# Masked attention: who adds the mask of two of the four score blocks

## The reference, cut to what matters

```
Q, K, V = proj(q, w_q), proj(k, w_k), proj(v, w_v)        # 16 heads of 16
scores = einsum('bhqd,bhkd->bhqk', Q, K) / sqrt(16)
scores = where(mask == 0, -1e9, scores)
attn = softmax(scores, axis=-1)
out = einsum('bhqk,bhkd->bhqd', attn, V) ... @ w_o.T
```

## Time and profile before

| | us |
|---|---|
| median of 3 runs | 1202.81 |
| lowest, highest | 1201.06, 1209.94 |
| the profiled execution, own time | 1203.75 |
| its span in the trace | 1202.0 |
| PE busy over the span | 1050.5 (87%) |
| DVE, ACT, POOL busy over the span | 659.1 (55%), 636.5 (53%), 200.0 (17%) |

### The profile page before, as it was taken

How to read it: one execution, slowest core, us unless ns; L and a number is a source line. 1 busy time by engine, 2 the same in 40 slices (tenths; PEclk the granted TensorE clock), 3 DMA queues, 4 the chain that set the end, 5 groups by cost and what they waited for, 6 DMA issues and landing times. The chain is left out here.

```text
span 1202.0 us, 21977 instructions
## 1 busy us (share of the span) xinstructions
PE 1050.5 (87%) x6945; PEld 658.6 (55%) x6979; DVE 659.1 (55%) x1993; ACT 636.5 (53%) x1275; POOL 200.0 (17%) x466
## 2 busy tenths in 40 slices
PE   7999999999978698999999991648999999987487
PEld 5555555655545498999999981213333333325254
DVE  4427888888856611211111104857666666775697
ACT  2447877877633232333333321526777777763697
POOL 0000000000000122222222210012222222330222
PEclk9958999999999898999999995869999999998798
DMA  5087898888749336666666644443111111100001
GB/s 184 1 306 293 321 330 322 316 321 324 290 141 360 136 110 226 223 222 219 225 218 222 220 140 153 152 147 91 47 49 46 47 46 46 47 20 10 0 32 40
DMA packets 75342, 199.55 MB, mean 166 GB/s; under 512 B 7880, under 2 KB 40904, under 8 KB 69256
## 3 DMA queue, kind: packets, MB, share of 16 engines
q1 hardware_dynamic: 71528, 188.45, 46.1%
q0 software_dynamic: 3744, 10.23, 2.2%
HBM read 134.82 MB, written 63.83 MB: 165 GB/s over the span
## 5 line engine op out<-in xcount | busy, mean ns | idle before, releaser
L784 DVE CUSTOM_DVE_ANT_0 unused<-mpsS,mask_bias 128x512 bf16<-128x512 f32 x256 | 172.0, 691 | 83.3 <-PE mpsS L717 82.9
L1526 ACT ACTIVATE hT<-ph,w 128x128 f32<-128x128 f32 x312 | 89.2, 369 | 207.7 <-PE ph L1500 207.7
L811 ACT ACTIVATE mPT<-mpsB 128x512 f32<-128x512 f32 x256 | 152.7, 597 | 81.1 <-PE mpsB L724 67.1
L1500 PE MATMUL ph<-xT,w 128*128 128x128 f32 x1248 | 152.1, 282 | 7.5 <-DMA w<-in_w1p 7.1
L1500 PEld LDWEIGHTS ph<-xT,w 128*128 128x128 f32 x1248 | 147.3, 197 | 10.8 <-issue 10.5
L1545 DVE TENSOR_TENSOR xn<-py,b 128x256 f32<-128x256 f32 x39 | 16.6, 425 | 247.4 <-PE py L1510 247.4
L1510 PE MATMUL py<-w,hT 128*128 x624 | 141.2, 379 | 0.7 <-DVE xn L1545 0.7
L659 ACT ACTIVATE scores<-scores,nm 128x512 f32<-128x512 f32 (+3 forms) x256 | 125.6, 557 | 9.8 <-DVE nm L624 9.8
L1510 PEld LDWEIGHTS py<-w,hT 128*128 128x128 f32 x624 | 115.6, 190 | 15.2 <-issue 1.1
L717 PE MATMUL mpsS<-mqk 96*128 96x512 bf16 x256 | 101.2, 397 | 19.5 <-DMA mqk<-packed 15.7
L611 DVE CUSTOM_DVE_ANT_0 scores<-psS,bias 128x512 f32<-128x512 f32 (+3 forms) x176 | 77.8, 487 | 54.6 <-PE psS L552 38.2
(11 more groups left out here) (267 smaller groups left out, 1621.5 us busy)
## 6 DMA issues: line engine op xcount, KB each, us to landing
w<-in_w1p SPq DMA_DIRECT2D x39, 1028.0 KB, 5.8
rel<-stage SPq DMA_DIRECT2D x44, 640.0 KB, 4.6
bias<-rel SPq DMA_DIRECT2D x44, 640.0 KB, 7.1
x<-rel SPq DMA_DIRECT2D x20, 640.0 KB, 6.8
mqk<-packed SPq DMA_DIRECT2D x64, 192.0 KB
w<-in_w2p SPq DMA_DIRECT2D x8, 1024.0 KB, 12.7
rel<-x SPq DMA_DIRECT2D x10, 640.0 KB, 3.2
rel<-mask_bias SPq DMA_DIRECT2D x10, 640.0 KB, 5.0
```

The costliest lines, as they stand in the source:

```text
L784: nc.vector.tensor_tensor_reduce(out=unused[:, i, :], in0=psS[i % 2][:, :], in1=mask_bias[:, i, :], scale=1.0, scalar=-3.0e38, op0=ALU.add ...
L811: nc.scalar.activation(PT[r][:, j, :], psB[j % 2][:, :], ACT.Exp, scale=1.0 / 4).then_inc(s_exp, 1)
L1500: mm = nc.tensor.matmul(ph[half][:, q * P:(q + 1) * P], w1[i][:, dk * F + f * P:dk * F + (f + 1) * P], xT[i][:, dk, :], start=(dk == 0), s ...
L1526: g = nc.scalar.activation(hT[i][:, f, :], ph[half][:, q * P:(q + 1) * P], ACT.Gelu, bias=w1[i][:, DK * F + f:DK * F + f + 1])
```

## The change

In block 0 of every head the mask is no longer added by PE. DVE reads the bank `psB[0]` after B0, adds `maskT` and writes the fp32 sum to a new SBUF tile `masked0`; ACT takes the exponential from there. In odd steps block 2 goes another way too: ACT copies the bank out to `masked2` after B2, POOL adds `maskT` in SBUF, and ACT takes the exponential of it at the head of the next (even) step, after that step's exponential of block 1. M0 of all 64 heads and M2 of the 32 odd heads are dropped. The exponentials are taken in the order 1, 0, 2, 3 and not 0, 1, 2, 3. Instead of the negation on POOL, the constant rows of the operand are -1.0 and the maxima are split as they are, in four instructions. The waits of B follow the new order: B2 waits for DVE's sum (`s_added`), B0 of an even step for ACT's copy (`s_copied`), B3 of an even step for the exponential of `masked2`.

```diff
--- before.py
+++ after.py
@@ -674,7 +674,9 @@
                 PT = [sb(ctx, f"mPT{r}", [P, NI, S]) for r in range(ROUND)]
                 unused = sb(ctx, "unused", [P, NI, S], BF16)
                 mx = sb(ctx, "mmx", [P, RING, NI])
-                neg = sb(ctx, "mneg", [P, RING, NI])
+                masked0 = sb(ctx, "masked0", [P, S])
+                masked2 = sb(ctx, "masked2", [P, S])
+                s_copied, s_hidden = sem("s_mcopied"), sem("s_mhidden")
                 zero = sb(ctx, "mzero", [P, NI])
                 rest = sb(ctx, "mrest", [P, RING, NI])
                 mp = sb(ctx, "mpieces", [P, RING, NI, 4], BF16)
@@ -684,9 +686,9 @@
                 psB = banks(ctx, "mpsB", 2)
                 psM = ctx.enter_context(nc.psum_tensor("mpsM", [P, 1024], BF16))
                 s_qk = [sem(f"s_mqk{r}") for r in range(RING)]
-                names = ("one", "smm", "soft", "mp", "mt", "row", "bmm", "exp", "seen")
+                names = ("one", "smm", "soft", "mp", "mt", "row", "bmm", "exp", "seen", "added")
                 s_seen_p = sem("s_mseenp")
-                s_one, s_smm, s_soft, s_mp, s_mt, s_row, s_bmm, s_exp, s_seen = (sem(f"s_m{n}") for n in names)
+                s_one, s_smm, s_soft, s_mp, s_mt, s_row, s_bmm, s_exp, s_seen, s_added = (sem(f"s_m{n}") for n in names)
                 block = ctx.enter_context(nc.Block())
 
                 @block.sync
@@ -718,14 +720,20 @@
                                                  start=True, stop=True).then_inc(s_smm, 1)
                             if late:
                                 m, slot, turn = late
-                                wait(pe, s_exp, NI * m + i - 1)
-                                nc.tensor.matmul(psB[i % 2][:, :], qk[slot][:, S + i * P:S + (i + 1) * P], qk[slot][:, 0:S],
-                                                 start=True, stop=False)
-                                nc.tensor.matmul(psB[i % 2][:, :], identb[:, :], maskT[:, i, :],
-                                                 start=False, stop=True).then_inc(s_bmm, 1)
+                                if i == 2:
+                                    pe.wait_ge(s_added, m + 1)
+                                elif r % 2 == 0 and i == 0:
+                                    wait(pe, s_copied, it * (ROUND // 2) + r // 2)
+                                else:
+                                    wait(pe, s_exp, NI * m + ((None, -1, None, 1), (-1, 0, None, 1))[r % 2][i])
+                                mm = nc.tensor.matmul(psB[i % 2][:, :], qk[slot][:, S + i * P:S + (i + 1) * P], qk[slot][:, 0:S],
+                                                      start=True, stop=(i == 0 or (i == 2 and r % 2 == 1)))
+                                if i in (1, 3) or (i == 2 and r % 2 == 0):
+                                    mm = nc.tensor.matmul(psB[i % 2][:, :], identb[:, :], maskT[:, i, :], start=False, stop=True)
+                                mm.then_inc(s_bmm, 1)
                             if rows and i == 1:
                                 m, slot, turn = rows
-                                pe.wait_ge(s_mp, 5 * (m + 1))
+                                pe.wait_ge(s_mp, 4 * (m + 1))
                                 wait(pe, s_row, m)
                                 for k in range(NI):
                                     tr = nc.tensor.transpose(psM[KP:KP + 3, k * P:(k + 1) * P], mp[:, slot, k, 0:3], identb[:, :])
@@ -748,42 +756,50 @@
                     def step(n, r, it):
                         if r % GROUP == 0 and (h := group_of(n, r, it, 0)):
                             vals.spread_values(pool, *h)
+                        if r % 2 == 1 and stage_of(n, r, it, 0):
+                            pool.wait_ge(s_copied, it * (ROUND // 2) + r // 2 + 1)
+                            nc.gpsimd.tensor_tensor(masked2[:, :], masked2[:, :], maskT[:, 2, :], ALU.add).then_inc(s_hidden, 1)
                         if h := stage_of(n, r, it, SOFT):
                             m, slot, turn = h
 
                             pool.wait_ge(s_soft, NI * (m + 1))
                             wait(pool, s_mt, m - RING + 1)
-                            wait(pool, s_mp, 5 * m)
+                            wait(pool, s_mp, 4 * m)
                             pool.sem_inc(s_seen_p, 1)
-                            nc.gpsimd.tensor_scalar(neg[:, slot, :], mx[:, slot, :], -1.0, 0.0, ALU.mult, ALU.add).then_inc(s_mp, 1)
-                            pool.wait_ge(s_mp, 5 * m + 1)
-                            nc.gpsimd.tensor_tensor(mp[:, slot, :, 0], neg[:, slot, :], zero[:, :], ALU.add).then_inc(s_mp, 1)
-                            pool.wait_ge(s_mp, 5 * m + 2)
-                            nc.gpsimd.tensor_tensor(rest[:, slot, :], neg[:, slot, :], mp[:, slot, :, 0], ALU.subtract).then_inc(s_mp, 1)
-                            pool.wait_ge(s_mp, 5 * m + 3)
+                            nc.gpsimd.tensor_tensor(mp[:, slot, :, 0], mx[:, slot, :], zero[:, :], ALU.add).then_inc(s_mp, 1)
+                            pool.wait_ge(s_mp, 4 * m + 1)
+                            nc.gpsimd.tensor_tensor(rest[:, slot, :], mx[:, slot, :], mp[:, slot, :, 0], ALU.subtract).then_inc(s_mp, 1)
+                            pool.wait_ge(s_mp, 4 * m + 2)
                             nc.gpsimd.tensor_tensor(mp[:, slot, :, 1], rest[:, slot, :], zero[:, :], ALU.add).then_inc(s_mp, 1)
-                            pool.wait_ge(s_mp, 5 * m + 4)
+                            pool.wait_ge(s_mp, 4 * m + 3)
                             nc.gpsimd.tensor_tensor(mp[:, slot, :, 2], rest[:, slot, :], mp[:, slot, :, 1], ALU.subtract).then_inc(s_mp, 1)
                     run_heads(pool, -LOAD, NBH - 1, step)
 
                 @block.vector
                 def _(dve):
                     for r in range(RING):
-                        nc.vector.memset(qk[r][KP:KM, S:2 * S], 1.0).then_inc(s_one, 1)
+                        nc.vector.memset(qk[r][KP:KM, S:2 * S], -1.0).then_inc(s_one, 1)
                     nc.vector.memset(zero[:, :], 0.0).then_inc(s_one, 1)
                     vals.clear(dve)
                     weights.clear(dve)
 
                     def step(n, r, it):
                         if h := stage_of(n, r, it, SOFT):
-                            m, slot, turn = h
-                            wait(dve, s_soft, NI * m)
-                            for i in range(NI):
+                            wait(dve, s_soft, NI * h[0])
+                        late = stage_of(n, r, it, 0)
+                        for i in range(NI):
+                            if h:
+                                m, slot, turn = h
                                 dve.wait_ge(s_smm, NI * m + i + 1)
                                 dve.sem_inc(s_seen, 1)
                                 nc.vector.tensor_tensor_reduce(
                                     out=unused[:, i, :], in0=psS[i % 2][:, :], in1=mask_bias[:, i, :], scale=1.0, scalar=-3.0e38,
                                     op0=ALU.add, op1=ALU.max, accum_out=mx[:, slot, i:i + 1]).then_inc(s_soft, 1)
+                            if late and i == 0:
+                                m = late[0]
+                                dve.wait_ge(s_bmm, NI * m + 1)
+                                wait(dve, s_exp, NI * m - 2)
+                                nc.vector.tensor_tensor(masked0[:, :], psB[0][:, :], maskT[:, 0, :], ALU.add).then_inc(s_added, 1)
                         if r % GROUP == 2 and (h := group_of(n, r, it, 2)):
                             vals.divide(dve, *h)
 
@@ -804,11 +820,24 @@
                         if late and r % GROUP == 0:
                             g, par = group_of(n, r, it, 0)
                             wait(act, vals.s_pv, NI * (g - 1))
-                        for j in range(NI):
-                            if late:
+                        for j in (1, 0, 2, 3):
+                            if j == 0 and r % 2 == 0 and (late or n == NBH) and not (isinstance(n, int) and n == 0):
+                                act.wait_ge(s_hidden, it * (ROUND // 2) + r // 2)
+                                nc.scalar.activation(PT[(r - 1) % ROUND][:, 2, :], masked2[:, :], ACT.Exp,
+                                                     scale=1.0 / 4).then_inc(s_exp, 1)
+                            if late and j == 2 and r % 2 == 1:
                                 m, slot, turn = late
                                 act.wait_ge(s_bmm, NI * m + j + 1)
-                                nc.scalar.activation(PT[r][:, j, :], psB[j % 2][:, :], ACT.Exp, scale=1.0 / 4).then_inc(s_exp, 1)
+                                wait(act, s_exp, NI * m)
+                                nc.scalar.copy(masked2[:, :], psB[0][:, :]).then_inc(s_copied, 1)
+                            elif late:
+                                m, slot, turn = late
+                                if j == 0:
+                                    act.wait_ge(s_added, m + 1)
```

(4 more changed lines are left out.)

## The result

The changed kernel takes 1217.33 us (median of 4 runs, 1215.52 to 1218.90) where the kernel before takes 1202.88 beside it: a ratio of **1.0104 [1.0077, 1.013]**, 9 to 16 us slower. The forecast was 1223. The profiled execution took 1215.52 and spans 1213.7 us, 11.7 more than before. Of these, 9.8 lie between the first S and the last B of the changed stage (295.2 us against 285.4). Another 1.5 lie ahead of it, where both programs are the same, and 0.4 behind it. The medians are further apart, 14.5 us, because the profiled execution of the changed kernel lies 1.8 under its median and that of the kernel before 0.9 over its own.

What follows compares the result with a forecast made beforehand. PE looked like the bound (99% busy), with 0.47 us of slack before S3; the instruction order was taken to decide. 31 pairs at 0.45 + 0.21 = 0.66 gave +20.5 on 1202.8, said as 1223, range 1208 to 1240.

Steps and rivals of the forecast that it cites:

- DVE's chain: DVE's addition between R0 and R1 delays S3 to 2.61; a step held there lasts 4.35, +0.21.
- The matmuls taken away are swallowed: PE's order: the 96 dropped matmuls, 21 us, gain nothing because they lay under DVE's chain.
- ACT in even steps: Five exponentials ahead of the row copy's end, which the next S0 awaits: even step 4.59, +0.45.
- A pair of steps: One even and one odd step of the changed stage together: 0.45 + 0.21 = 0.66 us longer.
- POOL hidden: POOL's addition ahead of the pieces, 1.20 long, puts T at 1.78; costs nothing, with 0.08 us of cover.
- (a): Rival: PE stays the bound and steps shrink by the matmuls dropped, 0.22 and 0.43; 1182, chance 0.10.
- (b): Rival: same chains at lower prices, part given back early in the stage at half clock; +4 to +12, 1210, chance 0.12.
- (c): Rival: POOL's addition takes about 2 us or DVE holds up its reads, T late; +43, 1246, chance 0.10.
- PE under 90% busy: Sign expected in the new trace: PE's busy share below 90%.
- PE idle before S0, ended by the row copy: Sign expected in the new trace: PE waits ahead of the S0 of odd steps until ACT's row copy.
- T about 0.5 late: Sign expected in the new trace: in even steps T comes about 0.5 late behind POOL.

Runs made afterwards that it cites:

- e1: The changed kernel with DVE's addition alone: M2 stays on PE for all heads, no copy-out, POOL addition or hidden E2; 1.0065 of the kernel before.
- e3: The changed kernel with a third PSUM bank for S, so that S3 waits for R0 alone; 0.9986 of the kernel before.
- e4: The changed kernel with DVE's addition narrowed to 128 of its 512 columns; 0.9973 of the kernel before.
- e5: The changed kernel with DVE adding block 3's mask after R3, M3 dropped, exponentials and row copy reordered, no odd half; 0.9924 of the kernel before.
- e2: The changed kernel with the odd half alone: PE adds block 0's mask again, exponentials in the order 0, 1, 2, 3; 0.9962 of the kernel before.
- e10: The changed kernel with the row copy one exponential earlier, ahead of E2, in even steps only; 1.0057 of the kernel before.
- e11: e3 with the row copy one exponential earlier in even steps only; 0.9951 of the kernel before.
- e7: The changed kernel with POOL's addition made twice, the first into a tile that nobody reads; 1.0227 of the kernel before.

## Why the prediction was right, and where it was not

**DVE's chain: right.** S3 was put at 2.61 and came at 2.55. The addition holds R1 back by 1.22 - 0.62 = 0.60, as taken. The rest is 0.06 that I took too much for the hand-off to PE: the 0.12 was read from the earlier trace rows, where the profile puts PE's idle time down to "issue" and not to DVE, so that row showed no hand-off. Steps go up by 0.16, not 0.21. e1, e3 and e4 agree: the addition alone gives the full effect, a third bank or a shorter addition takes this wait away. e5 agrees with it, though it moves more than the addition.

**The matmuls taken away are swallowed: right.** In the changed kernel they buy nothing in a regular step. e2 shows M2 worth its 0.22 where R1 is not delayed, and e5 shows the same of M3 in half of its steps.

**ACT in even steps: wrong, and it is the mis-sized term.** I had 0.67 from one SBUF exponential to the next instruction. The exponential lasts 0.62, but E0 starts 0.52 after the hidden one (933.95, 934.47) and E2 0.52 after E0. Even the hidden one starts 0.49 after E1, where I had 0.63. By these the row copy ends at 4.02 and not 4.47. The hand-off to PE was too short instead. My 0.12 came from the earlier trace rows, a step without S. B0 comes there 1.00 after W (1075.57 to 1076.57), just as S0 does in the earlier trace rows, so it hardly waited for the row copy. Where S0 does wait for the row copy, in the even steps of e3, it comes 0.24 after it; why it takes that long, no run isolates. So ACT's chain asks for 4.02 + 0.24 = 4.26, not 4.59, and lies 0.04 under the 4.30 of DVE's chain. I predicted +0.45; even steps are DVE's too, +0.16. e10 shows that ACT does not hold them, and e3, e4 and e11 that it is what comes next.

**The number: nearer than its terms, by luck.** A pair of steps was put at 0.66 and measured 0.32: even steps were 0.29 too dear and odd ones 0.05. The 49 regular steps grew by 7.8 us and the median by 14.5. The other 6.7 are in no term of mine: 2.7 came in the first ten steps, 1.9 outside the stage and 2.7 by which executions were profiled, less 0.7 at the stage's end. Without them 1223 would have been 12 us off and not 6.

**POOL hidden: right in effect, wrong in size.** The addition lasts 1.18 in the mean (predicted 1.20). The pieces were put at 1.58 of the even step and are out at 0.98, because POOL starts 0.08 after the copy-out and not 0.34, the copy-out itself is earlier by the short distances on ACT (3.02 and not 3.26), and the pieces start 1.12 after the addition and not 1.20 or more. The 0.20 from pieces to T was no hand-off either, since T was not waiting in that row. T was put at 1.78 and is on time at 1.19. The cover was ample only while DVE held odd steps at 4.30; at 3.91 (e3) T comes late.

**Rivals.** (a), the PE bound at 1182, is out: no run that leaves the addition between R0 and R1 comes near it, and even with the third bank an odd step takes 3.91 and not 3.70. (b) had one half right: prices were lower, by ACT's distances. Its other half did not occur, for the first ten steps, where the clock is low in part, gave nothing back and took 2.7 us more. Its +4 to +12 holds the stage's +9.8 and not the median's +14.5. (c) did not occur: POOL's addition would have had to take 1.7 us (1.16 + 0.54). Of the signs that I named, "PE under 90% busy", "PE idle before S0, ended by the row copy" and "T about 0.5 late" did not show, and even steps took 4.30 and not 4.6.

**What stays open.** The changed kernel, e1 and e10 have the same regular steps, 216.4 us for 49 of them, and ratios of 1.0104, 1.0065 and 1.0057. Their stages grew by 9.8, 8.5 and 7.4 us in the profiled executions; of the 2.4 us between the first and the last, 2.1 lie in the first ten steps. In the profiled executions the stage also starts anywhere from 793.0 to 796.8 us although nothing ahead of it was edited. One profiled execution of each kernel cannot tell how much of the 14.5 us beyond the 7.8 belongs to the change, and no run isolates it.

## What to carry to other kernels

A full engine in the windows does not say that its work is the bound: read, per ring of buffers, how many tenths of a microsecond lie between the last reader's end and the next writer's start, and put no instruction longer than that slack ahead of the last reader. Here the slack was 0.47 us and the addition 0.60. It cost 0.16 us a step and the dropped matmuls; behind the last read of the ring (e5) every step came out under the kernel before, by 0.13 to 0.22. When one wait is taken away, list those next in line with their distances before forecasting: here the row copy was 0.04 behind in even steps, so the third bank gained them 0.04 where odd steps gained 0.39.

## What the runs showed of the hardware

- In the changed kernel, exponentials of a 128x512 fp32 tile in SBUF last 625 ns in the mean, but one starts 0.49 us after the PSUM exponential ahead of it, and what follows one (another from SBUF, one from PSUM, the copy-out) starts 0.52 to 0.54 after it. Exponentials from PSUM last 596 ns, and the row copy follows one by 0.61. A chain summed from durations comes out too long.
- An addition on POOL of a 128x512 fp32 tile and a bf16 tile, both in SBUF, lasts 1178 ns in the mean, and the next POOL instruction starts 1.12 us after it. DVE's reductions beside it stay at 0.68 to 0.69.
- Hand-offs were 0.06 us from DVE's maximum to PE (934.64 to 934.70), 0.08 from ACT to POOL (948.56 to 948.64) and 0.05 from POOL to PE in e7 (959.34 to 959.39). From ACT's row copy to S0 it was 0.23 to 0.24 in e3 (950.73 to 950.96).
